# The store of the last tile as two transfers: 119 rows and 9 rows in place of 128

## The reference

```python
B_sel = B[adapter_ids]                              # 64 x 16 x 1024
A_sel = A[adapter_ids]                              # 64 x 1024 x 16
Bx = jnp.einsum('bni,bri->bnr', x, B_sel)
out = jnp.einsum('bnr,bor->bno', Bx, A_sel)
return x + out * 1.0
```

## Time and profile before

| what | value |
|---|---|
| median of three runs | 91.9 us (91.75 to 92.27) |
| the profiled execution | 92.17 us |
| its span, first to last instruction | 90.4 us |
| PE / DVE / ACT / POOL busy | 90% / 66% / 66% / 70% |
| DMA, mean over the span | 385 GB/s |
| read from and written to HBM | 17.83 MB, 16.78 MB |
| x and A, B, ids in; y out, by SP and ACT | queues q1 (SP) and q10 (ACT) |

### The profile page before, as it was taken

One profiled execution on the slowest core, in us unless ns is written; L12 is line 12 of the kernel. 1 busy time (PEld: TensorE's weight loads), 2 busy tenths in 40 slices (PEclk: granted clock), 3 DMA queues, 4 the chain that ended last, 5 costly groups with the idle time before them and its releaser, 6 DMA issues.

```text
span 90.4 us, 3583 instructions
## 1 busy us (share of the span) xinstructions
PE 81.4 (90%) x1451; PEld 61.7 (68%) x1451; DVE 59.7 (66%) x111; ACT 59.5 (66%) x154; POOL 62.9 (70%) x141
## 2 busy tenths in 40 slices
PE   3998999989999999999999999999999999989200
PEld 3997778748786878787878787786868687443000
DVE  0309968276595868777686959595959595999000
ACT  1339869939696969696969695968687776542200
POOL 6103992999999998979696979797969792800000
PEclk9999999999999999999999999999999999999955
DMA  1999999999999999999999999999999999997980
GB/s 27 315 401 419 415 406 415 401 413 406 406 410 410 402 424 413 406 419 417 413 421 413 422 413 410 415 422 406 421 417 413 421 410 397 406 383 314 408 335 24
DMA packets 9297, 34.82 MB, mean 385 GB/s; under 512 B 450, under 2 KB 962, under 8 KB 9282
## 3 DMA queue, kind: packets, MB, share of 16 engines
q1 hardware_dynamic: 7552, 27.79, 76.8%
q10 hardware_dynamic: 1730, 6.82, 18.6%
HBM read 17.83 MB, written 16.78 MB: 383 GB/s over the span
## 4 chain that ended last, share of the span: by engine, by line
PE 82%; DMA 6%; ACT 4%; issue 1%
PE t_bank L255 35%; PE bx_bank L268 21%; PE y_banks L288 18%; DMA x_all<-in_A 6%; PE y_banks L315 2%; PE t_bank L319 2%; ACT x_all L365 1%; PE bx_bank L319 1%; ACT b_table L369 1%; PE y_banks L242 1%; PE bx_bank L315 1%; ACT x_all L424 1%; ACT x_t L377 1%; PE t_bank L315 1%; PE bx_bank L242 0%
## 5 line engine op out<-in xcount | busy, mean ns | idle before, releaser
L465 DVE TENSOR_TENSOR x_all<-y_banks,x_all 128x1024 f32<-128x1024 f32 x29 | 35.5, 1225 | 15.4 <-PE y_banks L288 15.0
L377 ACT COPY x_t<-t_bank 128x512 f32<-128x512 f32 x64 | 34.4, 591 | 13.6 <-PE t_bank L255 12.8
L198 POOL CAST a_duo<-a_table 128x512 fp32r x64 | 36.6, 613 | 3.5 <-PE y_banks L288 1.8
L255 PE MATMUL t_bank<-ident,x_all 128*128 128x128 f32 x256 | 35.0, 280 | 0.4 <-ACT x_t L377 0.4
L255 PEld LDWEIGHTS t_bank<-ident,x_all 128*128 128x128 f32 x256 | 27.4, 141 | 7.4 <-issue 5.2
L188 POOL COPY b_duo<-b_table 128x256 f32 x64 | 22.8, 399 | 6.0 <-PE bx_bank L268 6.0
L268 PE MATMUL bx_bank<-x_t,b_duo 128*32 128x64 f32 x1024 | 20.8, 222 | 0.0
L268 PEld LDWEIGHTS bx_bank<-x_t,b_duo 128*32 128x32 f32 x1024 | 15.8, 109 | 5.4 <-issue 5.4
L288 PE MATMUL y_banks<-a_duo,bx_parts 64*128 64x512 f32 x112 | 17.3, 420 | 0.3 <-issue 0.3
L456 DVE TENSOR_TENSOR bx_parts<-bx_bank,bx_parts 32x64 fp32r<-32x64 f32 x64 | 14.1, 220 | 1.4 <-ACT bx_parts L392 0.3
L392 ACT CAST bx_parts<-bx_bank 32x64 fp32r<-32x64 f32 x64 | 13.0, 204 | 1.9 <-PE bx_bank L268 1.3
(11 more groups left out here) (31 smaller groups left out, 22.2 us busy)
## 6 DMA issues: line engine op xcount, KB each, us to landing
x_all<-in_x SPq DMA_DIRECT2D x5, 2048.0 KB, 28.6
out_y<-x_all ACTq DMA_DIRECT2D x3, 2048.0 KB, 15.4
x_all<-in_x SPq DMA_DIRECT2D x4, 1024.0 KB, 14.0
out_y<-x_all SPq DMA_DIRECT2D x1, 3072.0 KB, 14.0
out_y<-x_all SPq DMA_DIRECT2D x6, 512.0 KB, 4.7
x_all<-in_x SPq DMA_DIRECT2D x4, 512.0 KB, 7.2
out_y<-x_all SPq DMA_DIRECT2D x1, 2048.0 KB, 9.7
out_y<-x_all SPq DMA_DIRECT2D x2, 1024.0 KB, 6.7
```

The lines of the kernel that those rows point to most:

```text
L198: last = nc.gpsimd.tensor_copy(a_duo[duo % 2][:, k, :], a_table[:, bass.ds(adapters[k] * BANK, BANK)])
L255: last = nc.tensor.transpose(t_bank[unit % 2][:, c * P:(c + 1) * P], x_all[:, 2 * duo + tile, at:at + P], ident[:, :])
L377: nc.scalar.copy(x_t[duo % 2][:, half * HALF:(half + 1) * HALF, tile, :], t_bank[unit % 2][:, :].rearrange("p (c n) -> p c n", c=HALF)).th ...
L465: nc.vector.tensor_tensor(here, product, here, ALU.add).then_inc(y_drained, 1)
```

## The change

The store of tile 31 is issued in two parts: rows 0 to 118 of the tile, and rows 119 to 127. Each part adds 16 to `stored`, so the final wait asks for one transfer more. All other stores are issued as before.

```diff
     STORES = [(12, 18), (18, 22), (22, 24), (24, 26)] + [(t, t + 1) for t in range(26, TILES)]
+    LAST_STORE = [(0, 119), (119, P)]
...
                 if end == TILES:
                     sp.wait_ge(sum_copied, HALVES + 1)
-                sp.dma_start(out_rows[:, first:end, :], x_all[:, first:end, :]).then_inc(stored, 16)
-            sp.wait_ge(stored, 16 * (len(STORES) + len(STORES_BY_ACT)))
+                parts = [(0, P)] if end < TILES else LAST_STORE
+                for low, high in parts:
+                    sp.dma_start(out_rows[low:high, first:end, :], x_all[low:high, first:end, :]).then_inc(stored, 16)
+            sp.wait_ge(stored, 16 * (len(STORES) - 1 + len(LAST_STORE) + len(STORES_BY_ACT)))
```

## The result

The changed kernel takes 93.78 us, the median of four runs (93.36 to 94.20), against 91.94 us for the kernel before (four runs, 91.75 to 92.27): a ratio of 1.0204, 95% interval 1.0177 to 1.0230, or +1.9 us. The profiled execution took 94.06 us with a span of 92.3, so 1.9 us more than the span before.

What follows compares the result with a forecast made beforehand. DMA time at the tail was taken as the bound, the last engine setting the end: issues 0, ten more rows on the slowest of seven engines +1.55 us, span 91.95, time 93.5 us. Range 91.7 to 94.2.

Steps and rivals of the forecast that it cites:

- The bound: End of the run: after the last copy only DMA works, and the last engine to finish its share sets the end.
- The issues: SP's issues for tile 31: one transfer more, 0.33 us, hidden, so cost 0.
- the cover: Slack at the second issue while engines are busy with tile 30: 0.5 us; without it the cost would be 0.33 us.
- Seven engines: Store of tile 31: equal cut puts 17 rows on each of seven engines, 17 or 18 in place of 8: +1.55 us.
- Rivals 3 and 4: Tile 31's 119 rows spread nearly evenly, 91.9 to 92.1, chance 0.12; or all on one engine, 110, chance 0.01.
- The slowest among the seven: Store of tile 31: the latest engine is one of the seven loaded ones, +1.55 us; 7/16 = 0.44 by counting positions.
- the second rival: Tile 31: late engines lie outside the seven, a gain of 0.3 us, 91.6; chance 0.14 with the 0.35 us case.
- The pace of a row: Tile 31's rows on seven engines: 0.155 us each taken, 0.31 us as upper bound.
- shared reads: Tile 31: two engines reading the same place halve each other; for half the rows +1.3 us, kept for the range.
- The first rival: Tile 31: slowest outside the seven, a 0.8 us late engine inside: +0.5, 92.4; with shared reads up to 93.7; chance 0.27.

Runs made afterwards that it cites:

- 112 + 16: Changed kernel with tile 31 stored as 112 and 16 rows in place of 119 and 9: 92.03 us, ratio 1.0003.
- 114: Changed kernel with tile 31 stored as 114 and 14 rows in place of 119 and 9: 93.65 us, ratio 1.0205.
- 125: Changed kernel with tile 31 stored as 125 and 3 rows in place of 119 and 9: 94.57 us, ratio 1.0292.
- 120 + 8: Changed kernel with tile 31 stored as 120 and 8 rows in place of 119 and 9: 92.22 us, ratio 1.0034.
- the fourth stage: Behind the kernel's stores with tile 31 whole, rows 0 to 63 of tiles 24 to 31 stored again: 10.3 us.
- the second profile: The changed kernel run again without any further change: 94.03 us, ratio 1.0224.
- 124 + 4: Changed kernel with tile 31 stored as 124 and 4 rows in place of 119 and 9: 97.00 us, ratio 1.0541.
- The stages: Kernel with tile 31 whole, then seven rounds of repeated stores, each waited for before the next; run once: 5.0 us for 119 and 9 rows.
- the seventh stage: Behind the kernel's stores with tile 31 whole, that tile stored again as 127 and 1 rows: first completion after 21.1 us.
- the columns: Changed kernel, but tiles 26 to 31 each stored as columns 0 to 511 and 512 to 1023 of all rows: 92.25 us, ratio 1.0035.
- the halves by rows: Changed kernel, but tiles 26 to 31 each stored as rows 0 to 63 and 64 to 127: 93.45 us, ratio 1.0181.
- 127 + 1 kernel: Changed kernel with tile 31 stored as 127 and 1 rows in place of 119 and 9: 110.53 us, ratio 1.2005.

## Why the prediction was right, and where it was off

**The bound.** That the tail is DMA time and that the last engine sets the end: right. The last copy moved by 0.2 us only, and 112 + 16, the same work per engine, gave 1.0003.

**The issues.** Nothing for the second transfer: right by 112 + 16. Its issue took 0.69 us and not 0.33; the cover held.

**Seven engines.** Right: 14 completions after 88.12 us, and a share of 0.42 to 0.45 from 88.3 to 89.9. The equal cut gives 114, 125, 124 and 127 rows six, five, four and one engine, so with the second transfer 20, 8, 8 and 2 completions for tile 31, and SP's queue carries just these: 7556, 7544, 7544 and 7538 packets, of which 7536 are the others. For 112 + 16 and 120 + 8 it is 7568 and 7559, so 32 and 23. Rivals 3 and 4 are out.

**The slowest among the seven.** The forecast rested on this, at 0.44 by counting places. It was so: in both profiles of 119 + 9 the completion of tile 30 at 88.1 has a row right behind it. But no row of the kernel before placed that engine, so this part of the forecast was luck. The lateness seems to have a fixed home, as the second rival supposed, but within the seven, which rules out its gain. If it is one engine in all these runs, it has rows of tile 31 at 119, 114 and 125 rows and none at 124 and 127, so it is among five and not among four. Which of the 16 it is, no run shows. That the instruction packets make it late wasn't shown either.

**The pace of a row.** This is the term that was mis-sized. The prediction took 0.155 us, so 2.79 us for 18 rows, and kept 1.3 us of shared reads for the range. No run shows the source of those 1.3 us, two engines halving each other on half of the rows. What the runs show is 0.31 us a row for rows 0 to 63 with nearly all engines busy (the fourth stage, 204 GB/s over 0.95 x 16 engines), and in 119 + 9 slow rows of 0.21 to 0.70 us among rows of 0.155. In the changed kernel the slowest engine needed 3.4 us, from 88.13 to 91.51, and in the second profile 3.7. It began 0.2 us earlier than the forecast had it and ended 0.4 us later than the forecast's 91.1. That is the 0.35 us by which the span, 92.3, exceeds the forecast's 91.95, and about what the medians of 93.8 and 94.0 have over 93.5.

Slow rows hit the other engines harder: one that had ended tile 30 by 87.25 ended within 0.03 us of the slowest. So in this kernel two causes lead to nearly the same end, ten rows more on the late engine and slow rows on the others, and by this profile the execution would have ended at about the same time without a late engine among the seven. The first rival's upper figure, 93.7, was a better price than its lower one, and the forecast's number doesn't tell its case from that rival; the packets do. 124 + 4, which had no late engine and cost 5.0 us, shows this directly. The stages bear out how large the term is: 5.0 us for the cut with nothing late, where the prediction's two bounds were 2.8 and 4.1. Its reason for the upper bound, and for any row over 0.2 us, was shared reads. That is at most part of it: the one engine of the seventh stage had no other beside it and lost 1.4 us.

## What to carry to other kernels

Before cutting a store, write down how many rows each DMA engine gets, and add that to the time at which each engine becomes free: what counts is the latest sum. Keep a reserve for slow rows, which cost from nothing to about 3 us here. A number of rows that has only small divisors up to 16 loaded a few engines with everything: 119, 114, 125, 124 and 127 rows went to 7, 6, 5, 4 and 1. Cut by columns when a tile must go out in parts, and keep all 128 partitions in each transfer: the columns cost 0.3 us here and the halves by rows 1.7, and rows 0 to 63 alone went at 204 GB/s against 405. In the profile, divide GB/s by the DMA share: a high share with low GB/s, as 0.98 with 246 in 120 + 8 against 1.00 with 406 before, means slow rows, whatever their cause. Completions counted in narrow windows tell how many engines are late; which one is last takes following its packets one by one.

## What the runs showed that was not expected

The 127-row transfer has slow rows at its start, even with nothing queued and one engine alone: 1.4 us lost in the first 4 us of the 127-row stage and 1.3 us in the same time of the 127 + 1 kernel, and after that not one slow row in either, over 110 rows each. SP was held by the issue behind that transfer for 8.3 us (8.9 us in the 127 + 1 kernel); with more work behind on SP that would have a price of its own, by the author's estimate.
